# Projection of a Mamba-2 layer, first group: the low halves of the z weights on DVE, one behind each of eight products, in place of GpSimd

## What is computed

```python
h = rmsnorm(layernorm(x), ln1_w)                      # 2048 x 512
zxbcdt = h @ in_proj_w                                # 512 x 2576
z, xb, Bc, Cc, dt = split(zxbcdt)                     # 1024, 256, 256, 1024, 16 columns
xBC = silu(causal_depthwise_conv(xb|Bc|Cc, conv_w, conv_b))   # 4 taps
dt = softplus(dt + dt_bias)
... # chunked state space sum over (xBC, dt), giving y
y = rmsnorm(y * silu(z), norm_w) @ out_proj_w
```

## Time and profile before

| | us |
|---|---|
| median of 3 runs | 1599.17 |
| lowest, highest | 1597.35, 1601.76 |
| the profiled execution, its own time | 1602.53 |
| its span, first to last instruction | 1600.8 |
| TensorE busy in it | 1430.9 |
| DVE busy | 778.4 |
| GpSimd busy | 433.6 |
| mean granted clock of TensorE | 0.959 of full |

### The profile page before, as it was taken

The page is one execution under the profiler, slowest core; times in us unless marked ns, Lnnn a source line. Parts: engine busy times, 40 slices in busy tenths (PEclk is TensorE's granted clock), DMA queues, the critical chain, the costliest instruction groups (busy, mean ns, idle before and its releaser), DMA issues. The chain is left out here.

```text
span 1600.8 us, 20032 instructions
## 1 busy us (share of the span) xinstructions
PE 1430.9 (89%) x6643; PEld 1034.1 (65%) x6644; DVE 778.4 (49%) x1358; ACT 446.0 (28%) x925; POOL 433.6 (27%) x482
## 2 busy tenths in 40 slices
PE   5799999799999989999999999999720999999996
PEld 4577778566666658788888888888400555555553
DVE  5868778699999962433333332334544112121211
ACT  3444444555555541221221212211200111111110
POOL 1402121267677650111101111010116122222222
PEclk9899999899999989999999999999865999999998
DMA  8113125433233229100100001000694222223220
GB/s 186 53 72 119 74 79 158 165 116 109 93 111 121 93 94 363 44 27 17 36 13 26 26 15 38 0 0 1 211 362 176 73 77 86 85 84 91 79 86 15
DMA packets 92867, 147.12 MB, mean 92 GB/s; under 512 B 29182, under 2 KB 45566, under 8 KB 92800
## 3 DMA queue, kind: packets, MB, share of 16 engines
q1 hardware_dynamic: 79424, 119.92, 22.7%
q0 software_dynamic: 8800, 25.21, 4.7%
q10 hardware_dynamic: 4576, 1.13, 0.3%
HBM read 91.63 MB, written 58.27 MB: 94 GB/s over the span
## 5 line engine op out<-in xcount | busy, mean ns | idle before, releaser
L1388 PE MATMUL ff_bank<-ff_hT_hi,ff_w_hi 128*128 128x512 f32 x512 | 202.5, 396 | 4.4 <-DVE ff_w_lo L1358 3.2
L1388 PE MATMUL ff_bank<-ff_hT_hi,ff_w_lo 128*128 128x512 f32 x512 | 204.9, 400 | 0.0
L1388 PE MATMUL ff_bank<-ff_hT_lo,ff_w_hi 128*128 128x512 f32 x512 | 203.1, 397 | 0.0
L1836 PE MATMUL ex_bank<-w_gu,xT 128*128 x624 | 192.8, 462 | 1.2 <-ACT xT L1767 0.8
L1350 DVE TENSOR_TENSOR ff_prod<-ff_prod,ff_bank 128x512 f32<-128x512 f32 x64 | 44.0, 688 | 266.0 <-PE ff_bank L1388 248.8
L1284 POOL TENSOR_TENSOR ff_w_lo<-ff_stage,ff_w_hi 128x1024 fp32r<-128x1024 f32 (+1 forms) x24 | 56.4, 2353 | 409.6 <-ACT ff_w_hi L1337 409.0
L1836 PEld LDWEIGHTS ex_bank<-w_gu,xT 128*128 128x128 f32 x624 | 116.3, 191 | 60.4 <-issue 3.1
L1806 DVE SCALAR_TENSOR_TENSOR result_rows<-ex_bank,xs,result_rows 128x512 f32<-128x512 f32 x39 | 29.3, 751 | 256.1 <-DMA result_rows<-out_dram,xs 253.5
L599 PE MATMUL pj_bank<-hT_hi,w_in_hi 128*128 128x512 f32 x336 | 137.1, 408 | 12.0 <-DVE zst L525 6.0
L507 DVE SCALAR_TENSOR_TENSOR conv_acc<-raw,conv_w,conv_acc 128x512 f32<-128x512 f32 x144 | 113.9, 791 | 47.5 <-ACT raw L326 37.5
L599 PE MATMUL pj_bank<-hT_lo,w_in_hi 128*128 128x512 f32 x336 | 135.1, 402 | 0.0
(11 more groups left out here) (241 smaller groups left out, 2407.4 us busy)
## 6 DMA issues: line engine op xcount, KB each, us to landing
cv_rows<-cst SPq DMA_DIRECT2D x12, 1024.0 KB, 4.1
cv<-cv_rows SPq DMA_DIRECT2D x16, 768.0 KB, 4.3
sorted_rows<-blank SPq DMA_DIRECT2D x1, 10023.0 KB, 45.2
xs<-sorted_rows SPq DMA_DIRECT2D x39, 257.0 KB, 2.6
zs_rows<-zst SPq DMA_DIRECT2D x8, 1024.0 KB, 6.3
zs<-zs_rows SPq DMA_DIRECT2D x16, 512.0 KB, 5.2
w_gu<-in_L_ffn_Wg_dram SPq DMA_DIRECT2D x8, 704.0 KB, 10.5
w_gu<-in_L_ffn_Wu_dram SPq DMA_DIRECT2D x8, 704.0 KB, 11.3
```

Source lines behind the costliest of these rows:

```text
L1388: mm = eng.matmul(ps, w[a], x[b], start=first and i == 0, stop=last and i == 2)
L1836: mm = eng.matmul(ps[:, 0:EI], xT[v % 2][:, k, :], w_gu[:, i, bass.ds(e * KD + k, 1), :].rearrange("p a n -> p (a n)"), start=(k == 0), st ...
```

## The change

GpSimd's `split_z` and its calls behind products 4 to 7 (two each) are taken out. DVE gets the same function, with the same waits and the same semaphore, and calls it once behind each of products 4 to 7 (blocks 0 to 3 of z columns 0 to 511) and once behind each of products 9 to 12 (blocks 0 to 3 of columns 512 to 1023). On DVE it stands behind the taps, silu or gate and the other low half of the same product, and ahead of the softplus part, the statistics and the normalization. What TensorE waits for is as before.

```diff
@@ gpsimd
-            def split_z(a, k):
-                cols = slice(W_Z + a * 512, W_Z + (a + 1) * 512)
-                eng.wait_ge(s["w_hi"], KD + 2 * KD + a * KD + k + 1)
-                eng.tensor_tensor(w_lo[:, k, cols], w_raw[:, k, cols], w_hi[:, k, cols].bitcast(F32),
-                                  ALU.subtract).then_inc(s["wz_lo"], 1)
...
-                    if g == 0 and 4 <= n <= 7:
-                        for j in range(2):
-                            split_z((n - 4) // 2, 2 * (n - 4) % KD + j)
@@ vector
+            def split_z(a, k):
+                cols = slice(W_Z + a * 512, W_Z + (a + 1) * 512)
+                eng.wait_ge(s["w_hi"], KD + 2 * KD + a * KD + k + 1)
+                eng.tensor_tensor(w_lo[:, k, cols], w_raw[:, k, cols], w_hi[:, k, cols].bitcast(F32),
+                                  ALU.subtract).then_inc(s["wz_lo"], 1)
...
                     if g == 0 and 1 <= n <= KD:
                         split(2 * KD + n, n - 1, W_C + 512, W_C + 1024)
+                    if g == 0 and KD <= n < 2 * KD:
+                        split_z(0, n - KD)
+                    if g == 0 and 2 * KD < n <= 3 * KD:
+                        split_z(1, n - 2 * KD - 1)
```

## The result

The change makes the kernel 0.27% slower: ratio of the runs with the change to those of the kernel before, side by side, 1.0027, interval 1.0018 to 1.0035. The medians are 1603.5 us with the change and 1599.38 us before. I forecast 1602.5 us, 0.2% slower, "the same" by the bound of 0.3%; the range was 1599.0 to 1606.0. Three of the 26 executions took far longer (1886, 3795 and 4782 us) and are not in the ratio.

A forecast was written before the change was run, and what follows sets the result against it. TensorE, busy 89% of the span, was taken as the bound, so its stops in the projection count. One longer stop replacing two adds 3.3 us to the median 1599.17, giving 1602.5 us; range 1599.0 to 1606.0.

The forecast's parts named there:

- DVE's walk from 45.84: DVE's chain through products 4 to 7 in undisturbed intervals: fourth subtraction ends at 64.20, product 8 starts at 64.26, 10.65 us later.
- 7.2 us of mutual delay gone: DVE at products 4 to 7: without GpSimd's subtractions beside it, 7.2 us of stretching go, against 4 x 0.60 = 2.4 added.
- Rival (a): DVE's taps from product 4 stay stretched by ScalarE's copies; product 8 at about 71.4, time 1609.6 us; chance 5%.
- Product 8 at the low clock: TensorE behind the long stop: product 8 takes 5.2 us at the lower clock level, where 2.78 are needed.
- the lag of 3.3: Product 13 starts at 80.58 against 77.30, 3.3 us later; later stages take the shift whole; bounds 1.7 and 5.8.
- Rival (b): After 15 us without a matmul, products 8 and 9 both run at the lower clock; lag about 5.8, 1605.0 us; 11%.
- Second stop gone, second four covered: TensorE's stop at product 12 vanishes; the last subtraction ends at 86.0, product 16 needs it at about 89.9: cover 3.9 us.
- Nothing given back later: From product 15 on nothing adds to the 3.3 us, and no gain is taken from the 1.64 us stop at 98.35.
- (d): Rival: the 3.3 us are given back before the second group, in the turning of rows; no change, 1599.2 us; chance 5%.
- (c): Rival: TensorE's two stops at products 8 and 12 go and none comes; 14.4 us gained, 1584.8 us; chance 3%.
- my bound of 0.3%: Whole kernel: about 0.3% (4.8 us) is what a measurement can tell from no change; within it counts as the same, 76%.
- both stops and their replacement as one sum: TensorE between 49.0 and 77.30: 14.4 us lost on five products around two stops become 17.7 with one long stop.

## Why the prediction was right

- **DVE's walk from 45.84.** The subtraction ends were the core of it. I had product 8 at 64.26; it started at 63.50 + 0.73 = 64.23. Each of the four trains took 2.3 us, the statistics began at 64.10 (forecast 64.12). Undisturbed intervals from the second group of the same trace were good to 0.03 us over 18 us.
- **7.2 us of mutual delay gone.** Right, and shown: putting GpSimd's work back beside DVE lengthened the stop by 7.2 us. Rival (a), ScalarE's copies as the cause, is out.
- **Product 8 at the low clock.** I took 5.2 us; it took 68.41 - 63.50 = 4.91. This term was 0.3 too large and is the whole difference between the lag of 3.3 and the 2.96 of the trace. That it came so close is in part luck: in the four traces with a stop of over 11 us product 8 took 4.91, 4.94, 5.28 and 5.28 us, and behind the last two product 9 was 0.13 and 0.19 us longer as well. Rival (b), two products at the low clock, did not come: the level was back within product 8.
- **Second stop gone, second four covered.** No stop at product 12 or 16. The last subtraction ended at 84.20 + 0.68 = 84.88 and product 16 began at 88.90, a cover of 4.0 us (forecast 3.9). That the cover costs 0.6 when it is gone, the run with all four behind product 4 shows.
- **Nothing given back later.** The stop in the turning of rows is 1.86 in place of 1.64 us, and the lag at the second group is that at product 13. So (d) is out. (c) is out by the stop of 15.06 us, which is put down to DVE's fourth subtraction.
- **The size in timed runs** is 0.27%, 4.3 us of 1600, with 2.9 to 5.6 us in its interval; the trace's 2.96 lies at its lower edge. In the eight experiments the two readings differ by 0 to 1.2 us, either way (the first four alone: 6.9 us by the interval, 0.43% or 6.9 us by the ratio). Whether anything beyond the 2.96 is real, these runs can't tell. The call "the same" hung on my bound of 0.3%. It was too wide: the interval of the ratio is 0.17% from end to end and leaves out 1, so the runs do tell this change from none.

What the prediction left unsaid is that the change has two halves of opposite sign. I added up both stops and their replacement as one sum, which was right in size, but it hid that the second four alone were worth 3 us.

## What to carry to other kernels

Work that moves to another engine has to be costed by where it stands in that engine's order, against the time at which its consumer wants it; the engine's own balance (here 4.8 us better) says nothing on that. When an operation is stretched beside another engine's work, take its undisturbed duration from another stage of the same trace, walk the chain with those, and the new wait comes out nearly exact. And take a change with several placements apart before it is judged as a whole: one half of this one was a gain.

## What I had not expected of the hardware

The clock changes its level in a less regular way than I took it to. In two of the runs TensorE stopped at product 8 for the same time, 2.65 and 2.66 us, with the same work before. With all four behind product 4, the first three matmuls ran at the higher level, and the lower one set in only after the stop was over:

```profile
52.34 0.39 PE L601 MATMUL pj_bank<-hT_lo,w_in_hi 128*128 128x512 f32 x1
52.57 0.39 PE L601 MATMUL pj_bank<-hT_hi,w_in_lo 128*128 128x512 f32 x1
52.80 0.56 PE L601 MATMUL pj_bank<-hT_hi,w_in_hi 128*128 128x512 f32 x1
53.16 0.63 PE L601 MATMUL pj_bank<-hT_lo,w_in_hi 128*128 128x512 f32 x1
```

With the statistics moved as well, which is after this point in time, it had fallen when the first matmul came:

```profile
51.10 0.79 PE L601 MATMUL pj_bank<-hT_hi,w_in_hi 128*128 128x512 f32 x1 [2.66 <-DVE w_in_lo L443]
51.69 0.63 PE L601 MATMUL pj_bank<-hT_lo,w_in_hi 128*128 128x512 f32 x1
```

In these two the price came out equal all the same: product 8 took 4.45 us in both. Elsewhere it did not. The first product of the kernel is the same code in every run and stands behind the same stop of 1.56 us. It took 28.85 - 23.56 = 5.29 us in the trace of before and 4.20 in that of after (timeline of TensorE):

```profile
24.08 0.80 PE L600 MATMUL pj_bank<-hT_hi,w_in_hi 128*128 128x512 f32 x1 [1.56 <-DVE hT_lo L431]
...
28.28 0.39 PE L600 MATMUL pj_bank<-hT_hi,w_in_hi 128*128 128x512 f32 x1
```

It started 0.52 us later there and, with the product behind it, took 1.25 less: this is where the 0.73 us come from that I add. And product 8 stood behind 4.43 us in the kernel before and behind 4.44 with only the second four on DVE. It took 4.18 us in the one and 59.15 - 53.86 = 5.29 in the other:

```profile
59.15 0.59 PE L607 MATMUL pj_bank<-hT_hi,w_in_hi 128*128 128x512 f32 x1
```

A price for the clock taken from one stop of one trace can so be off by over 1 us, a third of the effect that this document is about.
